# A two-layer gated cross-attention and feed-forward kernel: products of the first part's last tiles cut around the transposes, a new order of loads and first products, and the growth of a factor moved on the GpSimd queue

## The reference, cut to what matters

```
x = x + tanh(g_xattn[0]) * attention0(layernorm(x), ctx)      # per row: a 16 x 16 softmax over 16 heads
x = x + tanh(g_ffn[0])   * (geglu_shared(layernorm(x)) + geglu_of_the_row's_expert(layernorm(x)))
x = x + tanh(g_xattn[1]) * attention1(layernorm(x), ctx)      # ordinary attention, 512 keys
x = x + tanh(g_ffn[1])   * butterfly_ffn(layernorm(x))

attention0: Q, K, V = rows @ W;  qk[i,j] = sum over heads h of Q[i,h] K[j,h] / 4   (i, j = 0..15)
            out[i,h] = sum over j of softmax(qk)[i,j] V[j,h];  then out @ Wo.T
geglu(x, w1, w2, w3) = (gelu(x @ w1) * (x @ w2)) @ w3        # 256 -> 1024 -> 256
idx = argmax(x @ Wg): each row goes to one of 8 experts
butterfly_ffn: expand 256 -> 1024, ten stages of 2 x 2 factors, gelu, ten stages, contract to 256
```

## Time and profile before

| what | value |
|---|---|
| median of 3 runs | 742.47 us (741.07 to 743.64) |
| the profiled execution's own time | 742.7 us |
| its span, first to last instruction | 740.9 us |
| mean granted clock of PE | 0.979 of full |
| PE, PE weight loads busy | 688.1 us (93%), 590.0 us (80%) |
| DVE, ACT, POOL busy | 619.9 us (84%), 411.1 us (55%), 426.9 us (58%) |

### The profile page before, as it was taken

One profiled execution on the slowest core, in us unless ns is written; L12 is line 12 of the kernel. 1 busy time (PEld: TensorE's weight loads), 2 busy tenths in 40 slices (PEclk: granted clock), 3 DMA queues, 4 the chain that ended last, 5 costly groups with the idle time before them and its releaser, 6 DMA issues.

```text
span 740.9 us, 12939 instructions
## 1 busy us (share of the span) xinstructions
PE 688.1 (93%) x4381; PEld 590.0 (80%) x4381; DVE 619.9 (84%) x911; ACT 411.1 (55%) x760; POOL 426.9 (58%) x304
## 2 busy tenths in 40 slices
PE   5739999999999899999999999999967899999998
PEld 4518888888888888577778888888856899989988
DVE  3888999999999846699999999999877867687654
ACT  2324554545545411457867778887533575456653
POOL 3898999999999950413999776669031301220000
PEclk9969999999999999999999999999989999999999
DMA  9501100011155211424155516010010101000000
GB/s 279 224 6 34 49 29 28 28 47 38 29 174 227 69 29 44 133 90 183 36 199 199 199 42 237 29 29 16 17 35 15 51 22 58 30 29 8 8 15 29
DMA packets 28642, 56.43 MB, mean 76 GB/s; under 512 B 3408, under 2 KB 24656, under 8 KB 27440
## 3 DMA queue, kind: packets, MB, share of 16 engines
q1 hardware_dynamic: 23408, 47.64, 18.2%
q0 software_dynamic: 1872, 5.11, 2.5%
q10 hardware_dynamic: 3312, 3.02, 1.2%
HBM read 48.55 MB, written 7.21 MB: 75 GB/s over the span
## 4 chain that ended last, share of the span: by engine, by line
PE 64%; DVE 12%; POOL 8%; issue 6%; ACT 5%; DMA 3%; SPq 1%; DVEq 0%; ACTq 0%; POOLq 0%
PE bank L742 29%; PE bank L751 20%; PE bank L1004 8%; PE bank L759 4%; POOL PRODV L624 4%; POOL PRODV L626 2%; DVE SLOT_r L2004 2%; DVE PRODV_r L2004 2%; DVE STC L2092 1%; ACT L1516 1%; DMA XS<-normal_rows,INV 1%; DMA COLS<-cols 1%; DVE bank L1625 1%; ACT XS L1516 1%; DVE NM L2142 1%
## 5 line engine op out<-in xcount | busy, mean ns | idle before, releaser
L624 POOL TENSOR_TENSOR PRODV<-SHARED 128x2048 f32<-128x2048 f32 x32 | 144.5, 4516 | 10.5 <-DVE bank L1697 5.6
L742 PE MATMUL bank<-ROWS,SLOT 128*128 128x128 f32 x1024 | 122.1, 278 | 0.4
L742 PEld LDWEIGHTS bank<-ROWS,SLOT 128*128 128x128 f32 x1024 | 117.5, 193 | 2.9 <-ACT G L1241 2.8
L718 POOL TENSOR_TENSOR RS<-VE,MHALF 128x2 f32<-128x2 f32 x16 | 13.1, 818 | 151.5 <-DVE VE L2099 151.5
L1616 DVE TENSOR_TENSOR PRODQ<-bank,SHARED 128x4096 f32<-128x4096 f32 x16 | 70.8, 4423 | 6.9 <-PE bank L742 6.1
L626 POOL TENSOR_TENSOR PRODV<-PRODV 128x1024 f32<-128x1024 f32 x32 | 74.8, 2339 | 2.5
L1625 DVE TENSOR_REDUCE bank<-PRODQ 128x256 f32<-128x4096 f32 x16 | 70.7, 4419 | 0.1
L641 POOL DMA_INDIRECT XS<-normal_rows,INV x23 | 29.0, 1260 | 65.1 <-PE bank L759 43.3
L2004 DVE TENSOR_TENSOR PRODQ_r<-SLOT,ROWS_r 128x1024 fp32r<-128x1024 f32 x44 | 62.2, 1445 | 0.0
L742 PE MATMUL bank<-SLOT,HA 128*128 128x256 f32 x256 | 60.1, 389 | 1.8 <-DVE HA L1811 1.8
L742 PEld LDWEIGHTS bank<-SLOT,HA 128*128 128x128 f32 x256 | 48.5, 194 | 15.6 <-DVE HA L1811 9.2
(11 more groups left out here) (286 smaller groups left out, 1919.7 us busy)
## 6 DMA issues: line engine op xcount, KB each, us to landing
SLOT<-wexp SPq DMA_DIRECT2D x9, 3072.0 KB, 11.9
ROWS<-xT SPq DMA_DIRECT2D x16, 128.0 KB, 2.2
SHARED<-ctxT SPq DMA_DIRECT2D x16, 128.0 KB, 2.3
X<-x SPq DMA_DIRECT2D x16, 128.0 KB, 2.5
normal_rows<-ROWS SPq DMA_DIRECT2D x16, 128.0 KB, 1.7
WET<-ctxT SPq DMA_DIRECT2D x4, 512.0 KB, 8.2
out<-X SPq DMA_DIRECT2D x16, 128.0 KB, 1.7
expert_rows<-YS ACTq DMA_DIRECT2D x12, 128.0 KB, 1.7
```

Source lines behind the costliest of these rows:

```text
L624: gp.tensor_tensor(o, pr, v, ALU.mult).then_inc(s["av_prod"], 1)
L742: last = pe.matmul(dst, lhs(k), rhs(k), start=(k == 0), stop=(k == chunks - 1))
```

## The change

**Loads and first products.** Before, SP loaded WQ0, x and context of tile 0 transposed, WKV0, X; then tile 1, WO0, WG and GATE, the coefficients, four weights and COLS. Now the context and WKV0 come before x; X of tile 0 comes in two DMAs of 64 rows; WO0, WG and GATE are issued behind tile 2's loads. PE makes the key half of tile 0 (bank 6) ahead of its queries and the value half (bank 4) behind; ACT copies the key half first, and DVE's first `scores` waits for that alone. `guarded_first` of tile 0 comes behind the first `scores`, and POOL's `first_root` of tile 0 behind `grown_up`. The tanh of the gates moves on ACT from step 0 to the end of step 1. In steps 1 to 3, which have no down product, `queries` comes right behind the keys and values.

**Pieces.** `up_half` and `down_rows` can be issued in parts. `down_rows` waits for HA's first half before its product 0, and for the second half only before its product 4, in the loop too. In step 16 and in `drain` pieces stand between a transpose and the product that needs its copy.

**Tail.** POOL no longer waits for the whole normed row of tile 14 between the halves of tile 15. `grow_down` runs right behind the last value products, with the last `second_root` ahead of its last step; its scratch moves to the key and value buffer, and PLACE and TOPS move into PRODQ's space. The last down product is cut 7 + 1: the eighth stands behind the transpose of the first expert tile, and the wait for `y_added` of all tiles stands before the second half of the first expert's up product.

```diff
             sp.dma_start(WQ0[:, :, :], wq0.rearrange("(k p) n -> p k n", p=P)).then_inc(wq_in, 16)
-            load_turned(0, 0)
+            sp.dma_start(CTX[:, 0, :, :], ctxT[:, 0:P].rearrange("(k p) t -> p k t", p=P)).then_inc(w_in, 16)
             sp.dma_start(WKV0[:, :, :], wkv0.rearrange("(k p) n -> p k n", p=P)).then_inc(w_in, 16)
-            sp.dma_start(X[:, 0, :], x[0:P, :]).then_inc(tile_in[0], 16)
+            sp.dma_start(XT[0], xT[:, 0:P].rearrange("(k p) t -> p k t", p=P)).then_inc(tile_in[0], 16)
+            for h in range(2):
+                rows = slice(h * P // 2, (h + 1) * P // 2)
+                sp.dma_start(X[rows, 0, :], x[rows, :]).then_inc(tile_in[0], 16)
             load_tile(0, 1)
-            for w, src in ((WO0, wo0), (WG, wg)):
-                sp.dma_start(w[:, :, :], src.rearrange("(k p) n -> p k n", p=P)).then_inc(wg_in, 16)
-            sp.dma_start(GATE[:, :], gates.partition_broadcast(P)).then_inc(wg_in, 16)
...
             load_tile(1, 0)
+            for w, src in ((WO0, wo0), (WG, wg)):
+                sp.dma_start(w[:, :, :], src.rearrange("(k p) n -> p k n", p=P)).then_inc(wg_in, 16)
...
                 if (t0 := of(0)) is not None and first(t0, 1):
+                    grown_up()
                     first_root(t0)
-                    grown_up()
...
                             second_root(T - 2)
-                            gp.wait_ge(s["xn2_ready"], 3 * (T - 1))
...
             sweep_a(gp, step)
-            second_root(T - 1)
+            gp.wait_ge(coef_in[1], 16)
+            v = COEF[1][:, 0:16]
+            for k in reversed(range(LOW - 1)):
+                if k == 0:
+                    second_root(T - 1)
+                w = (KV[:, 0, :] if k % 2 else EC)[:, 0:1024 >> k]
+                grow_down(k, v, w)
+                v = w
...
-            def down_rows(t4):
+            def down_rows(t4, start=0, stop=KF):
 
                 n4 = num(t4)
-                pe.wait_ge(s["mult_done"], 2 * n4 + 2)
-                if not first(t4, 1):
-                    pe.wait_ge(s["y_added"], n4)
-                product(PB[2][:, 0:D], lambda k: HA[:, k, :], lambda k: W3[:, k, :], KF, s["y_done"])
+                for k in range(start, stop):
+                    if k == 0:
+                        pe.wait_ge(s["mult_done"], 2 * n4 + 1)
+                        if not first(t4, 1):
+                            pe.wait_ge(s["y_added"], n4)
+                    if k == 4:
+                        pe.wait_ge(s["mult_done"], 2 * n4 + 2)
+                    last = pe.matmul(PB[2][:, 0:D], HA[:, k, :], W3[:, k, :], start=(k == 0), stop=(k == KF - 1))
+                if stop == KF:
+                    last.then_inc(s["y_done"], 1)
...
                 attended(b)
+                up_half(a, 1, 0, 1)
                 out_rows(b)
-                up_half(a, 1)
+                up_half(a, 1, 1)
                 normal_rows(b)
+                down_rows(a, 0, 2)
                 gate(b)
-                down_rows(a)
-                up_half(b, 0)
+                down_rows(a, 2)
+                up_half(b, 0, 0, 7)
                 attended(c)
+                up_half(b, 0, 7)
                 out_rows(c)
                 up_half(b, 1)
                 normal_rows(c)
+                down_rows(b, 0, 1)
                 gate(c)
-                down_rows(b)
+                down_rows(b, 1)
                 ranks()
...
                 inverse()
-                down_rows(c)
+                down_rows(c, 0, 7)
...
                 if t1 is not None:
                     scores(t1)
+                    if first(t1, 1):
+                        guarded_first(t1)
```

More of the change, by code:

```diff
@@ L767, in _, with up_half @@
             W3 = SLOT[:, 2, 2 * KD * F:WS].rearrange("p (c d) -> p c d", c=KF)
-            def up_half(t3, hf):
+            def up_half(t3, hf, start=0, stop=8):
                 n = 2 * num(t3) + hf
-                for bank, w, done, free in ((PB[6], W1, "h1_done", "gelu_done"),
-                                            (PB[7], W2, "h2_done", "mult_done")):
-                    if not (first(t3, 1) and hf == 0):
+                for i in range(start, stop):
+                    bank, w, done, free = ((PB[6], W1, "h1_done", "gelu_done"),
+                                           (PB[7], W2, "h2_done", "mult_done"))[i // 4]
+                    q = i % 4
+                    m = 4 * hf + q
+                    if q == 0 and not (first(t3, 1) and hf == 0):
                         pe.wait_ge(s[free], n)
-                    for q in range(4):
-                        m = 4 * hf + q
-                        product(bank[:, q * P:(q + 1) * P], lambda k: w[:, k, m * P:(m + 1) * P],
-                                lambda k: X2T[:, t3[1], k, :], KD, s[done] if q == 3 else None)
+                    product(bank[:, q * P:(q + 1) * P], lambda k: w[:, k, m * P:(m + 1) * P],
+                            lambda k: X2T[:, t3[1], k, :], KD, s[done] if q == 3 else None)
             def attended(t3):
@@ L965, in expert_up @@
                 n = num(t1)
+                if n == 0:
+                    down_rows(tile(T - 1), 7)
                 slot = held_for.pop(n)[0] if n else 0
@@ L968, in expert_up @@
                 for hf in range(2):
+                    if n == 0 and hf:
+                        pe.wait_ge(s["y_added"], T)
                     if not first(t1, 1):
@@ L1736, in step @@
                     row_max(t1)
-                if t0 is not None:
+                if t0 is not None and not first(t0, 1):
                     guarded_first(t0)
```

80 lines of the change are left out of this document (43 added, 37 removed).

## The result

Five executions of the changed kernel took 733.0, 733.7, 735.4, 736.3 and 739.3 us, a median of 735.4; before has 741.3 over five. Six more executions of the same kernel, beside others of before, gave 737.2 (0.9942, interval 0.9928 to 0.9956), so that all eleven have a median of 736.6. The terms of the forecast were not right, as the profiles and the runs with one part undone show.

The account below looks back on a forecast made before the run. Inside the loop PE, DVE and POOL were taken as full, PE fullest, so only time before and after it could move. Terms 1.5 + 0.5 + 1.5 + 0.5 + 1.1 = 5.1 us gave 737.5 us, range 735.8 to 740.0.

Parts of the forecast that it names:

- The last down product: Expert transposes no longer wait for the eighth product and y_added: 1.1 us, bounds 0.5 to 1.4; earlier third fetch at most 0.35.
- The start: Before the loop: COLS lands 0.7 us earlier, pair products perhaps at full clock 0.8; 1.5 us, bounds 0 and 2.9.
- Step 3: Tile 3's queries leave the path between tile 0's transposes and up products: 0.5 us, bounds 0 and 1.2.
- The loop: Steady steps with PE full: 0 gained, at most 0.8 us lost through the second wait in `down_rows`.
- the slower rival: The mid-product wait drains PE's queue in every tile: 744.7 us or more, chance 0.04.
- Step 16: Down product starts on HA's first half, but the transposes still wait for ACT's row: 0 us.
- the wait on POOL: Tile 15's second half starts right behind `second_root`, the wait for the normed row removed: 1.5 us, bounds 0.6 and 1.6.
- pieces before the ranks: One down product behind tile 15's second transposes lies under ACT's copy, not ahead of the ranks: 0.5 us, bounds 0 and 0.5.
- The clock falls in the drain: Rival: PE idle in step 16 drops the clock and costs 2 us, giving 739.6; chance 0.10.
- Only the tail arrives: Rival: pair products stay at half clock, COLS lands unchanged, step 3 gives nothing; gain 3.1 us, 739.5; chance 0.17.
- the head: Changes before the loop and in step 3: forecast 1.5 and 0.5 us.
- the tail: POOL's removed wait, pieces before the ranks and the cut last down product: 1.5 + 0.5 + 1.1 = 3.1 us.

Follow-up runs that it names:

- growth_back: Changed kernel with the down growth put back behind the first two fetches, ahead of the third, with scratch, PLACE and TOPS as before: 742.4 us.
- growth_only: Kernel before with only the growth's move, between the last half tile's sums and the fetches: 738.6 us, ratio 0.9951.
- before_fill: Kernel before plus 30 unused identity products in step 3, ahead of the transposes of the first normed row: 739.6 us.
- head_only: Changed kernel with growth, drain, POOL's wait and last down product of before, so only the new loads, first products and queries: 742.3 us, ratio 0.9995.
- down_whole: Changed kernel with the last down product whole and the wait for y_added back ahead of the expert transposes: 737.4 us.
- queries_late: Changed kernel with the queries of tiles 2 and 3 back behind the transposes and tile 1's behind the pair products: 736.5 us.
- after: Changed kernel, nothing undone, as first measured: median 735.4 us over five executions; the profiled execution is the longest of the five.
- fill_3: Changed kernel plus 27 unused identity products in step 3 alone, ahead of the transposes of the first normed row: 735.4 us.
- pool_wait: Changed kernel with POOL's wait for the normed row back ahead of tile 15's second half: 739.0 us.
- drain_whole: Changed kernel with the drain's products whole in the old order and the last step's down product whole ahead of the transposes: 737.9 us.
- again: Changed kernel, nothing edited, executed six more times: 737.2 us.
- fetch_first: Changed kernel with the growth behind the third fetch instead of ahead of all fetches: 738.4 us.
- no_tail: Changed kernel keeping new head, queries and growth order, with drain, POOL's wait and last down product of before: 738.4 us.
- fill_16: Changed kernel plus 7 unused identity products in the last step alone, between the first six down products and the transposes: 736.6 us.
- fill: Changed kernel plus unused identity products ahead of transposes, 27 in step 3 and 7 in the last step: 732.5 us, ratio 0.9886.

## Why the prediction was right or wrong

**The step that failed** is the last sentence of "The last down product": "With the growth gone from behind it, the third fetch goes out earlier; [...] DVE is full around there: 0, at most 0.35". Its move alone gives 3.4 us, and without it the rest of the change gives nothing (growth_back 742.4 against 741.4). I priced it by the 0.35 us that PE waited in one execution in which PE itself was late: the half clock at 298 to 300 us had put the transposes 1.2 us back. With the transposes on time PE waits 2.0 to 2.6 us for that fetch, 0.4 to 0.5 for DVE's splitting, and the products behind run at half clock for a while, 2.9 to 3.7 us in all. "DVE is full around there" was no cover, since PE waits for the fetch itself. The two terms that I added, the earlier transposes and the growth, are one chain: late transposes hide the price of the late fetch. growth_only keeps the old tail and still gives 3.4, so most executions of before probably had their transposes on time, as before_fill's profile has; no other execution of before has a trace to show it.

**The start, 1.5.** COLS's gain came, the clock's mostly did not. The first pair product, which waits for COLS, begins at 16.6 us on the mean of the twelve profiles with the changed start and no products ahead of the pair products, and at 17.4 on that of three with the old start (before, growth_only, before_fill; 16.7 to 18.1): 0.8 where I had 0.7. In the twelve, POOL's first value product lies between 21.64 and 25.10, mean 23.5; before and growth_only have 24.35 and 25.94, before_fill 23.57, mean 24.6. The difference of 1.1 lies within my bounds (0 to 2.9), but three profiles of the old order are few for it. The clock was up when COLS landed in two of the twelve, head_only and down_whole; their first pair product took 1.99 us and they have the two earliest starts, 21.64 and 21.86. In the other ten it took 3.29 to 3.78 and the start came at 22.89 or later. I gave that chance one half.

**Step 3, 0.5.** It did not come. "To mult" takes 37.4, 37.9 and 38.0 in the old order (before, growth_only, queries_late) and 37.3 to 38.8, 38.3 on the mean, in ten profiles of the new one: nothing gained, perhaps 0.5 lost. What the saving turned into is in the traces: tile 0's first up products, which I let begin earlier at unchanged length, take 4.3 to 4.9 us in those three and 5.15 to 6.65 in the ten. A likely reading is that the queries, 1.9 us of products at half clock, had helped to bring the rise before the up products; the runs do not show it, since the rise also moves between executions of one order. queries_late, which undoes it, costs nothing (736.5). Start and step 3 together make about 0.6 by these means; the medians say 0.2 (medians of different comparisons, in which before's own moved by 0.6).

**The loop, 0.** Right, within 0.1 us over twelve steps; the slower rival is out.

**Step 16, 0; the wait on POOL, 1.5; pieces before the ranks, 0.5.** "To INV" is 51.9 to 52.2 us in the old order and 49.9 to 50.0 in the new one with the clock up: 2.1 gained against my 2.0. The rival "The clock falls in the drain" is not an alternative to this but happens in part of the executions: in five of the eight profiles with the pieces and without idle products in that place (after, growth_back, fill_3, down_whole, pool_wait). It fell in drain_whole too. It costs 1.6 to 3.3 us, where I had 2. I gave it 0.10 and argued against it with a wait of 1.75 us; the new idle time was longer, 2.08 to 2.14. But its length does not decide it: the clock stayed up behind 2.08 and 2.14 us in again and fetch_first, and fell behind 1.27 in drain_whole. pool_wait costs 2.4 by the median and not 1.5. Its profile is one in which the clock fell, and against those of after, growth_back and fill_3, where it fell by as much (up products of 4.4 to 4.6 us), its "to INV" is 1.2 longer (52.77 to 51.58); the rest I can't place.

**The last down product, 1.1.** The distance in the trace is right (4.87 to 3.65), its reason is not. Whole, the product is late only at half clock: at full clock there the five other profiles with it whole (head_only, no_tail, growth_only, before_fill, down_whole) have 3.59 to 3.67, and cut it is 3.65 in after at half clock too. Undone alone it costs 0.8 on the median, not clear of the spread.

**The rival "Only the tail arrives"**, to which the Trainium skill's section on oscillation spoke, had the mechanism of the head right in most profiles (the clock stayed down there in ten of twelve) but not the time: the head's terms gave 0.2, the tail 1.8, the growth 3.4, in sum 5.4 where I had 2.0, 3.1 and 0, 5.1. That my sum of 5.1 is so near is luck: a term put at nothing made up for others that did not come.

Left open: why growth_back lies 5.8 us above the changed kernel by the median, when "part 2" explains 2.9 of it; the other executions have no trace, but their mean clock is lower (0.972 to 0.981, against 0.979 to 0.984). And why fill_3 and fill_16 add up to so little of what fill gives; their nine executions each are spread over 7.8 and 5.1 us, so it may be no more than that. And whether the load of the weights is what makes the late fetch slow to land.

## What to carry to other kernels

Before an engine's late work is priced at the wait seen in one profile, ask whether its consumer was itself late there; if anything else in the change brings the consumer forward, the wait grows at least by that. Look as well at what else is on the DMA queues when a late transfer goes out. When work is moved out from between two waits to save its time, look at the granted clock behind it: at half clock the saving may not arrive. Products that compute nothing, laid into idle stretches ahead of a critical burst until just before it begins, made 5.3 us here, and five executions lay within 1.4 us; pool_wait's six lay within 0.7 without any such products, at a median of 739.0, so the smaller spread is not theirs alone.

## What the runs showed of the hardware

The clock was up or down at the same place in different executions of code that is the same there: at the pair products (1.99 or 3.3 to 3.8 us for eight records), in step 16 (3.82, 4.42, 5.67 us for 32) and behind 27 idle products that ended 1.48 us ahead of the transposes in one profile (fill, clock stayed) and 1.25 ahead in the other (fill_3, clock fell); behind 30 that ended 1.21 ahead it stayed (before_fill). So the idle time just ahead does not decide it alone. The first gather of the third part took 3.4 to 4.0 us to land in most profiles and 5.2 and 5.5 in before and queries_late, in kernels that differ in nothing near it. A fetch of 128 rows took 3.2 to 3.4 us to land with nothing large beside it and 8.6 to 9.5 around the issue of a 3 MB load. DVE's splitting of two 128x1024 pieces takes 2.36 us alone and up to 4.56 beside POOL's growth step, which grows from 2.13 to 3.00.
